# Two cross-attention layers on one core: GpSimd and ScalarE work between the layers put at other places

## The reference, cut to what matters

```
# layer 0, one head
qn, kvn = layer_norm(x) * g_q + be_q, layer_norm(ctx) * g_kv + be_kv
q, k, v = qn @ Wq.T + bq, kvn @ Wk.T + bk, kvn @ Wv.T + bv
x = x + softmax(q @ k.T) @ v @ Wd.T + bd
# layer 1, eight heads of width 256; K and V from the raw context
s = where(mask, (x @ Wq_h) @ (ctx @ Wk_h).T / 16, -inf)
o = sum_h softmax(s) @ (ctx @ Wv_h) @ Wo_h + x
out = layer_norm(o) * gamma + beta
```

## Time and profile before

| | |
|---|---|
| median of three runs | 500.2 us |
| the profiled execution, its own time | 499.98 us |
| its span in the trace | 498.0 us, 7565 instructions |
| TensorE busy | 473.5 us (95%) |
| VectorE busy | 332.2 us (67%) |
| ScalarE busy | 291.5 us (59%) |
| GpSimd busy | 245.6 us (49%) |
| first matmul starts at | 11.1 us |

### The profile page before, as it was taken

How to read it: one execution, slowest core, us unless ns; L and a number is a source line. 1 busy time by engine, 2 the same in 40 slices (tenths; PEclk the granted TensorE clock), 3 DMA queues, 4 the chain that set the end, 5 groups by cost and what they waited for, 6 DMA issues and landing times.

```text
span 498.0 us, 7565 instructions
## 1 busy us (share of the span) xinstructions
PE 473.5 (95%) x2424; PEld 395.6 (79%) x2424; DVE 332.2 (67%) x679; ACT 291.5 (59%) x482; POOL 245.6 (49%) x153
## 2 busy tenths in 40 slices
PE   1999999999999999999999999999999999999994
PEld 0777787777878888888888888888888888888893
DVE  5999866476685658565756585658566765673666
ACT  4667376458665656566656565656566655556332
POOL 4636763555855363637271717272726363454004
PEclk9999999999999999999999999999999999999998
DMA  8313013677865656565656475647474746572002
GB/s 289 122 45 127 1 32 117 214 208 227 245 220 177 211 170 211 170 211 169 211 169 220 159 218 161 229 151 243 137 253 131 248 140 222 147 226 66 0 2 84
DMA packets 50774, 81.97 MB, mean 165 GB/s; under 512 B 5792, under 2 KB 38976, under 8 KB 50624
## 3 DMA queue, kind: packets, MB, share of 16 engines
q1 hardware_dynamic: 41792, 50.16, 34.5%
q10 hardware_dynamic: 8960, 31.54, 16.9%
HBM read 49.16 MB, written 32.51 MB: 164 GB/s over the span
## 4 chain that ended last, share of the span: by engine, by line
PE 84%; DVE 7%; ACT 3%; issue 2%; POOL 2%; DMA 2%; SPq 0%; DVEq 0%; POOLq 0%; ACTq 0%
PE ps_scores L626 31%; PE ps_o L658 6%; PE ps_o L651 6%; PE ps_o L650 6%; PE ps_o L657 6%; PE ps_o L652 6%; PE ps_task L574 3%; PE ps_task L573 3%; PE ps_task L572 3%; DMA ring<-in_weights_a 2%; PE ps_out L572 2%; PE ps_out L573 2%; PE ps_out L574 2%; PE ps_out L744 1%; PE ps_turn L642 1%
## 5 line engine op out<-in xcount | busy, mean ns | idle before, releaser
L514 POOL TENSOR_TENSOR probs_t_lo<-probs_t_lo,probs_t_hi 128x1024 fp32r<-128x1024 f32 (+1 forms) x75 | 146.7, 1967 | 176.6 <-ACT probs_t_hi L1018 176.6
L1018 ACT ACTIVATE probs_t_hi<-probs_t_lo 128x1024 fp32r<-128x1024 f32 (+1 forms) x75 | 64.6, 880 | 36.9 <-DMA probs_t_lo<-scratch 34.9
L626 PE MATMUL ps_scores<-key_hi,q_hi 128*128 128x512 f32 x144 | 57.8, 402 | 1.3 <-DVE neg_scores L1352 0.8
L1339 DVE RECIPROCAL row_inv<-row_sum 128x1 f32<-128x1 f32 x72 | 11.3, 159 | 71.1 <-PE ps_scores L626 68.4
L650 PE MATMUL ps_o<-probs_t_hi,val_hi 128*128 128x512 f32 (+1 forms) x144 | 56.6, 393 | 1.1 <-issue 0.9
L626 PE MATMUL ps_scores<-key_rem,q_lo 128*128 128x512 f32 x144 | 56.6, 393 | 0.5 <-DVE q_lo L1434 0.3
L626 PE MATMUL ps_scores<-key_lo,q_hi 128*128 128x512 f32 x144 | 56.6, 393 | 0.0
L626 PE MATMUL ps_scores<-key_rem,q_hi 128*128 128x512 f32 x144 | 56.6, 393 | 0.0
L626 PE MATMUL ps_scores<-key_hi,q_lo 128*128 128x512 f32 x144 | 56.4, 392 | 0.0
L651 PE MATMUL ps_o<-probs_t_lo,val_hi 128*128 128x512 f32 (+1 forms) x144 | 56.3, 391 | 0.0
L658 PE MATMUL ps_o<-probs_t_lo,val_rem 128*128 128x512 f32 (+1 forms) x144 | 56.2, 392 | 0.0
(11 more groups left out here) (256 smaller groups left out, 1096.9 us busy)
## 6 DMA issues: line engine op xcount, KB each, us to landing
probs_t_lo<-scratch SPq DMA_DIRECT2D x240, 128.0 KB, 3.0
scratch<-neg_scores ACTq DMA_DIRECT2D x30, 512.0 KB, 3.4
scratch<-probs ACTq DMA_DIRECT2D x30, 512.0 KB, 3.7
ring<-in_weights_a SPq DMA_DIRECT2D x9, 512.0 KB, 4.9
ring<-in_weights_b SPq DMA_DIRECT2D x9, 512.0 KB, 5.3
ring<-in_keys_t SPq DMA_DIRECT2D x4, 512.0 KB, 3.4
ctx_raw<-in_context SPq DMA_DIRECT2D x2, 768.0 KB, 8.9
ring<-in_context SPq DMA_DIRECT2D x16, 96.0 KB, 2.6
```

What stands on the lines that cost most here:

```text
L514: nc.gpsimd.tensor_tensor(pt_lo[b][:, t, k, :], pt_lo[b][:, t, k, :].bitcast(f32), moved_part(j, k).bitcast(f32), ALU.subtract).then_inc(m ...
L626: last = pe.matmul(ps_scores[:, n], left, right[:, n], start=(i == 0), stop=(i == len(passes) - 1))
L1018: act.activation(moved_part(j, k), pt_lo[b][:, t, k, :].bitcast(f32), ACT.Copy)\
```

## The change

ScalarE gets `round_vals0` of both batches at earlier places and `round_values(PC_V00, 0)` in two halves. GpSimd gets `split_vals0(0)` in the first batch's part, and the bias additions in two groups of four. VectorE sums the shift of batch 1 for three tiles at the old place and for the fourth behind the four subtractions. The computation is the same.

```diff
+            def bias_resid(b):
+                pool.wait_ge(centred, b * LN_TILES + QT)
+                for t in range(b * QT, (b + 1) * QT):
+                    nc.gpsimd.tensor_tensor(resid[:, t, :], resid[:, t, :], outb, ALU.add).then_inc(biased, 1)
...
                 if b == 1:
                     split_weights(HI_OF[PC_A1], 0)
-                    split_vals0(0)
+                    pool.wait_ge(outb_made, 1)
+                    bias_resid(0)
                 rsqrt(b, 0, KT, 2 * b + 2)
                 pool.wait_ge(kv_rows_loaded, 16)
                 bias_tiles(b, range(CTX_HALF, KT), done + QT, ctx_normed[1])
                 if b == 0:
                     split_weights(HI_OF[PC_B0], 1)
-
-            pool.wait_ge(centred, LN_TILES + QT)
-            pool.wait_ge(outb_made, 1)
-            for t in range(BATCHES * QT):
-                nc.gpsimd.tensor_tensor(resid[:, t, :], resid[:, t, :], outb, ALU.add)\
-                    .then_inc(biased, 1)
+                    split_vals0(0)
+
             split_vals0(1)
+            bias_resid(1)
             split_keys(PC_KA0, 0)
...
             round_queries(T_Q0b, 0, 1, 0)
+            round_vals0(0)
             exp(-1, 0)
...
             exp(-1, 2)
-            round_vals0(0)
             round_chunk(1, 0)
...
                 round_chunk(1, c)
+            round_vals0(1)
             round_outputs(-1, 0)
             exp(-1, 4)
-            round_vals0(1)
             round_a(T_A1, 0, -1.0 / 16)
...
             round_probs(-1, 6)
-            round_values(PC_V00, 0)
+            round_values(PC_V00, 0, (0,))
             exp(-1, 7)
             round_queries(T_QH, 0, 0, 1)
             round_queries(T_QHb, 0, 1, 1)
             round_probs(-1, 7)
+            round_values(PC_V00, 0, (1,))
...
             ln_scale_context(1)
-            sum_shift(1, range(QT))
-            finish_shift(1)
+            sum_shift(1, range(QT - 1))
             for c in range(2, CHUNKS):
                 split_chunk(1, c)
+            sum_shift(1, range(QT - 1, QT))
+            finish_shift(1)
             dve.wait_ge(shift_made, 2)
             split_outputs(-1, 0)
```

## The result

The changed kernel took 502.31 us in the median of 5 runs (501.99 to 503.25), against 500.19 (499.96 to 500.55): 1.0038 times as long, 95% interval 1.0024 to 1.0052. The profiled run is the median one, 502.31 us with a span of 500.1 us, so 2.1 us more span than before. A second set of 8 runs gave 501.53 (500.61 to 502.50) against 500.07, 1.0028 [1.0017, 1.0039]. The forecast was 500.9, +0.7 us, with a range up to 502.3, so the first median stands at the very edge of it. By the bound of 0.2% the kernel is slower, which the forecast gave a chance of 0.26. Direction and place were right. The size was a third of the 2.1 us of the first set and half of the 1.5 us of the second.

The account below looks back on a forecast made before the run. VectorE was taken to bound stretches ahead of 84 us, with TensorE busy without a break behind. +1.92 us at 26 us and -1.24 by 80 us gave +0.68, so 500.9 us against 500.2, range 498.8 to 502.3.

Parts of the forecast that it names:

- What bounds the kernel: VectorE is late in stretches ahead of 84 us; TensorE runs without a break behind, so earlier changes reach the end whole.
- Part 1: Batch 0's values early: at 26 us GpSimd's subtraction goes ahead of the first `finish_shift`, delaying TensorE's next scores by +1.92 us.
- cap at the 1.00 us: At 26 us, if no wait exceeded the trace's longest extra one, 1.00 us, the early values would cost 0.9 us less.
- Part 2: Bias additions in two groups: batch 1's norm ends 0.94 us earlier, TensorE's transposes start 0.41 earlier.
- Part 3: Divided shift sums of batch 1: scores of step 4 can start 0.67 us earlier, but their minimum comes 0.50 later.
- the race: Near 57.8 us, whether GpSimd's subtraction or VectorE's second `finish_shift` goes first; GpSimd was taken, by a 0.04 us margin.
- Part 4: Copies out of ScalarE's way: TensorE -0.14 us at 66.44, -0.40 at 73.17, -1.24 at the last turn near 80 us.
- The sum: +1.92 us at 26 us and -1.24 by 80 us make +0.68 us, lasting to the end.
- all of +1.92 stays: The delay at 26 us is kept whole, since VectorE has no slack up to 36.5 nor from 46 to 58.4 us.
- The range: Eight in ten from 498.8 to 502.3 us.
- rival 3: At 26 us GpSimd's second subtraction also precedes `finish_shift`: +1.9 us, 502.1; lasting transfer delay would look the same; chance 0.13.
- Rival 2: The waits at both `finish_shift` don't occur and each edit works: -2.38 or in part -1.2 us, 497.8 to 499.0; chance 0.16.

Follow-up runs that it names:

- e11: Changed kernel with batch 0's values rounded and split at their old places and batch 1's shift sums in one piece again: 497.38 us, 0.9951 of before.
- e7: Changed kernel with batch 0's values at their old places and GpSimd waiting for the second `finish_shift` before batch 1's split: 498.05 us, 0.9958 of before.
- e1: Kernel before with only batch 0's values rounded and split at the new early place: 503.08 us, 1.0061 of before.
- e8: Changed kernel with `round_values(PC_V00, 0)` in one go again, both halves before the last exponentials: 501.82 us, 1.0042 of before.
- e9: Changed kernel with ScalarE's spill at the 159 us step held back until the fetch has landed: 501.64 us, 1.0025 of before.
- e10: Changed kernel with batch 1's four shift sums and `finish_shift` in one piece ahead of the key subtractions again: 500.41 us, 1.0001 of before.
- e12: Changed kernel with TensorE's product before the scores of step 1 made three times, filling its wait: 502.88 us, 1.0047 of before.
- after: The changed kernel itself, whole change against the kernel before: 502.31 us in the first set, 501.53 in the second, each set with a profile.
- e6: Changed kernel with GpSimd waiting for the second `finish_shift` before it splits batch 1's values: 500.59 us, 1.0004 of before.
- e4: Kernel before with batch 0's values rounded and split early, GpSimd waiting for `finish_shift` before the split: 501.92 us, 1.0035 of before.
- e3: Changed kernel with GpSimd waiting for `finish_shift` before each of the two value splits: 498.89 us, 0.9974 of before.
- e2: Changed kernel with batch 0's values rounded and split at their old places: 499.20 us, 0.9982 of before.

## Why the prediction was right, and where it was not

- **What bounds the kernel:** right up to 160 us. What was won or lost ahead of 84 us was still there at 160 us in every profile, within 0.15 us.
- **Part 1:** right. 1.92 forecast, 2.03 and 1.99 measured. The Trainium skill ("SBUF — State Buffer", section "Who interferes with whom") says that whichever of the two engines issues first keeps the shared ports for its whole instruction while the other is fully blocked; the trace agrees, 2.22 to 2.27 us of `finish_shift` in every collision, and no cap at the 1.00 us that I had weighed against it.
- **Part 2:** right in kind. The transposes came 0.62 us sooner against the rest, for 0.41.
- **Part 3:** its sum was right, its reason was not. The scores of step 4 came 0.90 us sooner (forecast 0.67) and VectorE lost the race. But the divided sums gave nothing for it: measured from the scores of step 1, those of step 4 come 0.89 us sooner than before with the sums whole (e11) and 0.88 with them divided and gated (e7). Part 2 had already ended the norm early enough: in e11 and e7 TensorE starts these scores without idle time. So dividing only brought `finish_shift` into the race, and with the race won it was no gain either.
- **Part 4:** right at 66.41, 0.2 short at 73.17 (1.71 us of lag for 1.52), and the last turn gained 1.09 to 1.12 against the 1.24.
- **The sum:** +0.68 for +0.87 to +0.94 at 80 us.
- **The step that failed** is "all of +1.92 stays" and "what is won or lost ahead of 84 us goes to the end whole", with everything that the lag might set off counted 0: a lag at 80 us was to be the lag at the end. "TensorE's idle time behind 84 us changes by more than a few tenths" was named as what would make the forecast wrong, and in the first profile it did. Two things can come on top, and neither had a term. One is the clock: in four of the seven profiles in which TensorE idled 2.0 us at 30 us and the wait was not filled (e1, e8, e9, e10) it fell to its lower level for 3.4 us, at 1.3 us each. In the six without that idle time it never did, nor in e12. The other is a fetch that lands 0.9 us later when it meets a spill. In the profiles of after, e6, e8 and e12, which show this at 159 us, the lag grew by 0.9 to 1.2 us between 160 and 200: in e12 all at 167 us, in the others 0.4 to 0.5 there and 0.4 to 0.7 at 194, the part that is only argued to follow. The first profile of after has this second thing alone: 0.94 + 1.07 is its 2.0 us. The second profile has neither. Of its late 0.9 us, 0.65 come at 435 to 439 us, behind a fetch on which ScalarE went on 4.56 us behind the last issue, for 3.41 before, with the spill 1.3 us behind in both. So a fetch can land late without such a meeting too, and why it does is open.
- **The range:** that it reached the result is luck. Its upper end was put there for rival 3, whose mechanism did not happen.
- **The rivals:** rival 3's time came in the first set (502.1), in its profile by the last clause, a lasting delay of transfers, and not by the mechanism. Rival 2's "-2.38" is what the change holds once the waits are gone: -2.23 and -2.69 in e7 and e11. The chance of "slower" was too low for want of the two knock-on terms, which added time wherever they occurred.

**What stays open.** How the median comes about. The clock fits the groups in the times of e8 and e10, though a mean clock of 0.994 doesn't prove a fall at 30 us: e6's profile has it without one. In e8 the two longer runs, at 0.992 and 0.993, are below every profile without a fall. It doesn't account for e12, where it was taken away and the time did not fall, nor for e4, whose median is 1.6 us above before with 0.6 in the profile. Why the fetch meets the spill in some executions and not in others is known only in part. The lag at 80 us alone doesn't decide it, as after's two profiles show. The slow third issue took 1.70, 1.46 and 1.77 us in after, e6 and e8, where the two met, and 1.17 in after's second profile. But it took 1.46 and 1.50 in e9 and e11 too, so it doesn't decide it alone either.

## What to carry to other kernels

When GpSimd's work is moved into a gap where it is idle, look at which small instructions of VectorE that work in SBUF (here a `tensor_scalar` of four numbers) lie within its duration, since the shortest instruction on the critical path pays for the longest one beside it. A wait that lets VectorE's small one go first, or a place where nobody stands, is worth more than the earlier start (e3, e7, e11). And a new wait of 2 us on TensorE is not priced by its own length alone: leave room upward for the clock behind it and for transfers that meet otherwise.

## What was not expected of the hardware

- The hand-over goes one by one. At 28.6 us GpSimd had its next instruction ready when the first ended, and the waiting `finish_shift` still came first: it ended 0.03 us behind the first, and the next took its usual 1.27 us. The margin that decides is small: at 57.9 us (e2) and 60.1 us (after) the last sum ended 0.04 us ahead of `finish_shift`, and GpSimd, some 0.15 us ahead of it, went first.
- 2.0 us of idle time on a TensorE that was busy before can bring the granted clock down to 1.2 GHz for 3.4 us. In the profiles with that idle time it fell where the clock had risen to full at 15.9 us or later (15.89, 16.10, 16.24, 17.08) and not where it had at 14.83, 15.13 or 15.63. So small a difference at the start of the kernel goes with 1.3 us later.
- When a spill is issued close to a fetch, the order decides. Over all fourteen profiles, of the places behind 150 us where ScalarE waited for a fetch: with the spill 0.2 to 0.8 us behind the fetch's last issue it went on 2.8 to 3.2 us behind that issue (18 of 21, the rest 3.4 to 3.6); with 0.1 us or less, 3.9 to 4.5 (6 of 6); with the spill 0.2 or 0.3 us ahead of it, 4.4 (2 of 2); with the spill 0.5 us ahead, 4.2 to 5.8 (53 of 53). Ahead of 150 us there are six more places with the spill 0.2 to 0.7 us behind, and there it took 4.1 to 5.4; in five of them a load of weights was still in flight when the fetch began, in the sixth loads of context were issued right behind it. The places differ in more than the order, so the cleanest comparison is the one step at 159 us above. The Trainium skill ("DMA: Bandwidth & Descriptors", section "Issuing engines are not separate DMA queues") says that transfers of different issuing engines run on the same 16 DMA engines and interleave. These numbers agree, and show besides that at the step at 159 us a lead of 0.22 us was enough for the fetch to lose nothing (2.99 us, as with a lead of 0.39).
